# A one-core decoder layer on Trainium2: when x, residuals and weights are asked for at the seams of its stages

## The reference

```python
def reference(x, ctx_1024, mask_BxS2_bf0, ...):
    # two Mamba-2 passes (forward, and over flipped time), joined by a projection:
    #   h = LN(x) + concat(fwd, bwd) @ proj_w.T + proj_b;   attn = LN(h) * ln_w + ln_b
    x = x + _L0_attn_ref(_layernorm(x, axis=-1), ...)
    # 16 heads of 32, queries from LN(x), keys and values from ctx, causal and padding masks
    x = x + _L0_xattn_ref(_layernorm(x, axis=-1), ctx_1024, ctx_1024, mask_BxS2_bf0, ...)
    # mixture of 16 experts: gated q, k, v of width 64, causal attention, gated output
    x = x + _L0_ffn_ref(_layernorm(x, axis=-1), ...)
    return x

def _layernorm(x, axis=-1, eps=1e-05):
    m = jnp.mean(x, axis=axis, keepdims=True)
    v = jnp.var(x, axis=axis, keepdims=True)
    return (x - m) / jnp.sqrt(v + eps)
```

## Time and profile before

| | us |
|---|---|
| median of 3 runs | 4629.91 |
| lowest and highest | 4629.33 and 4635.51 |
| the profiled execution's own time | 4637.03 |
| its span in the trace | 4635.0 |
| mean granted TensorE clock | 0.95 of full |

### The profile page before, as it was taken

One profiled execution on the slowest core, in us unless ns is written; L12 is line 12 of the kernel. 1 busy time (PEld: TensorE's weight loads), 2 busy tenths in 40 slices (PEclk: granted clock), 3 DMA queues, 4 the chain that ended last, 5 costly groups with the idle time before them and its releaser, 6 DMA issues. The chain is left out here.

```text
span 4635.0 us, 72509 instructions
## 1 busy us (share of the span) xinstructions
PE 4139.6 (89%) x26456; PEld 3072.3 (66%) x26456; DVE 3183.5 (69%) x6884; ACT 1664.6 (36%) x3487; POOL 1004.4 (22%) x597
## 2 busy tenths in 40 slices
PE   6999999997898898988858888888898789999998
PEld 5776776764666666656546666566576467777787
DVE  5888888884588887878646646546547476666664
ACT  3333333432333333333226626537437321111111
POOL 1333333242244454444500000000000100000000
PEclk8999999998899999999979999999999899999999
DMA  2111011102011110110143143143142220000000
GB/s 102 35 40 38 26 39 38 40 22 99 17 42 35 45 42 32 49 42 32 36 150 100 42 150 98 61 139 86 62 144 70 78 71 28 28 28 28 28 33 19
DMA packets 144917, 265.89 MB, mean 57 GB/s; under 512 B 25140, under 2 KB 31288, under 8 KB 144568
## 3 DMA queue, kind: packets, MB, share of 16 engines
q1 hardware_dynamic: 144568, 261.27, 17.0%
HBM read 164.58 MB, written 88.08 MB: 55 GB/s over the span
## 5 line engine op out<-in xcount | busy, mean ns | idle before, releaser
L1665 ACT ACTIVATE xa_src<-xa_s,xa_mn 128x896 f32<-128x896 f32 (+7 forms) x512 | 376.7, 738 | 221.8 <-DVE xa_mn L1749 218.4
L1749 DVE TENSOR_REDUCE xa_mn<-xa_s 128x1 f32<-128x896 f32 (+7 forms) x512 | 374.7, 751 | 55.4 <-PE xa_s L1842 49.6
L1848 PE MATMUL xa_gen<-xa_ident,xa_src 128*128 128x128 f32 x2304 | 331.4, 281 | 25.2 <-DVE xa_kq L1774 11.2
L72 PE MATMUL ff_wb<-ff_w_hi,ff_st_hi 128*128 128x512 f32 x768 | 322.5, 420 | 15.7 <-DVE ff_parts L2353 9.9
L1612 POOL TENSOR_TENSOR xa_res<-xa_res,xa_bor 128x512 f32<-128x512 f32 x32 | 40.4, 1267 | 1298.7 <-DMA xa_res<-after_mamba_dram 1298.7
L73 PE MATMUL ff_wb<-ff_w_hi,ff_st_lo 128*128 128x512 f32 x768 | 309.4, 403 | 0.0
L74 PE MATMUL ff_wb<-ff_w_lo,ff_st_hi 128*128 128x512 f32 x768 | 309.3, 403 | 0.0
L1848 PEld LDWEIGHTS xa_gen<-xa_ident,xa_src 128*128 128x128 f32 x2304 | 253.4, 144 | 66.3 <-issue 55.1
L1757 DVE COPY xa_pT<-xa_gen 128x512 f32<-128x512 f32 (+3 forms) x352 | 185.9, 528 | 129.8 <-PE xa_gen L1848 125.8
L1203 PE MATMUL mb_ib<-mb_wc,mb_yT 128*128 128x512 f32 x512 | 268.4, 673 | 1.8 <-DVE mb_y L974 1.0
L2121 POOL TENSOR_TENSOR ff_mixed<-ff_at,ff_rw 128x1024 f32<-128x1024 f32 x32 | 60.9, 1904 | 877.3 <-DVE ff_at L2381 877.3
(11 more groups left out here) (511 smaller groups left out, 11409.4 us busy)
## 6 DMA issues: line engine op xcount, KB each, us to landing
xa_qa<-xa_q_dram SPq DMA_DIRECT2D x384, 64.0 KB, 2.0
xa_q_dram<-xa_kq SPq DMA_DIRECT2D x32, 512.0 KB, 2.8
xa_k_dram<-xa_kq SPq DMA_DIRECT2D x32, 512.0 KB, 2.8
xa_ka<-xa_k_dram SPq DMA_DIRECT2D x192, 64.0 KB, 2.0
xa_st<-xa_k_dram SPq DMA_DIRECT2D x192, 64.0 KB, 2.0
mf_xg<-in_x_dram SPq DMA_DIRECT2D x16, 512.0 KB, 5.4
turned_dram<-mf_xt_hi SPq DMA_DIRECT2D x16, 512.0 KB, 2.6
turned_dram<-mf_xt_lo SPq DMA_DIRECT2D x16, 512.0 KB, 4.0
```

Source lines behind the costliest of these rows:

```text
L72: nc.tensor.matmul(out, w_hi, x_hi, start=first, stop=False)
L1665: a_.activation(pq[:, hh, 0:w], s1[g, i, hh][:, 0:w], ACT.Exp, scale=-1.0, bias=mn[:, i % 2, hh:hh + 1], accum_out=sums[:, i // QT, i % QT ...
L1749: v_.tensor_reduce(mn[:, i % 2, hh:hh + 1], s1[g, i, hh][:, 0:(i + 1) * P], AX.X, ALU.min).then_inc(mx_ready.sem, 1)
L1848: last = tr(ps[:, n * P:(n + 1) * P], pq[:, hh, j * P:(j + 1) * P], ident[:])
```

## The change

Four things change, and no matmul is added or removed.

1. Backward pass, last tile only: its two residuals go to the unused half 0 of `xtok` (function `residual`), and SP asks for them as soon as tile 30's have landed and tile 30 no longer needs that half, and not once tile 30's output is finished.
2. Cross attention, the head of a batch: `load_x`, `stats`, `ln` and `xn` go by halves of 4 tiles. `mask` moves behind them. In the first batch the mask is asked for between the q weights and the k weights. The 1/sqrt chain is run twice per batch on 4 columns.
3. Cross attention, the end of a batch: the first half of x is asked for ahead of output 2, the second ahead of output 3, and the two halves are normed among the outputs. Before `kq` 0 and `kq` 8, PE waits for the low parts of the first 4 tiles alone, and before `kq` 1 and `kq` 9 for the rest.
4. The experts' stage: SP asks for the first two blocks of weights ahead of `load` 1.

```diff
+        def residual(c):
+
+            spare = xtok[:, N % 2, :]
+            return (spare[:, 0:D], spare[:, D:2 * D]) if c == N - 1 else (partb[:], xres[:])
...
-                    wait(sp, out_ready, c - 1)
-                    sp.dma_start(partb[:], part[b, rows, :]).then_inc(res_loaded.sem, 16)
-                    sp.dma_start(xres[:], x_in[b, rows, :]).then_inc(res_loaded.sem, 16)
+                    def load_residual(c):
+                        b, rows = rows_of(c)
+                        for t, src in zip(residual(c), (part, x_in)):
+                            sp.dma_start(t, src[b, rows, :]).then_inc(res_loaded.sem, 16)
+
+                    if c < N - 1:
+                        wait(sp, out_ready, c - 1)
+                        load_residual(c)
+                    if c == N - 2:
+                        wait(sp, base_ready, inner(c))
+                        wait(sp, res_loaded, 2 * c + 1)
+                        load_residual(N - 1)
                 wait(sp, out_ready, c)
...
         def head():
+            yield "load_x", 0
+            yield "load_x", 1
+            for half in range(2):
+                for t in range(QT):
+                    yield "stats", half * QT + t
+                yield "ln", half
+                for t in range(QT):
+                    yield "xn", half * QT + t
             yield "mask", 0
-            yield "load_x", 0
-            for t in range(NT):
-                yield "stats", t
-            yield "ln", 0
...
             yield "load_x", 0, 0
+            yield "load_x", 0, 1
             yield "fetch", 0, 0
+            yield "load_mask", 0, 0
             yield "fetch", 0, 1
...
+                yield "load_x", it + 1, 0
+                yield "o", it, QT - 2
+                yield "load_x", it + 1, 1
+                yield "o", it, QT - 1
+                yield "load_mask", it + 1, 0
+                yield "o", it, QT
+                ahead = [n for n in head() if n[0] != "load_x"]
+                cut, end = ahead.index(("xn", 0)), ahead.index(("ln", 1)) + 1
+                for what, n in ahead[:cut]:
                     yield what, it + 1, n
-                for t in range(QT, QT + 2):
-                    yield "o", it, t
-                for what, n in ahead[2:]:
+                yield "o", it, QT + 1
+                for what, n in ahead[cut:end]:
                     yield what, it + 1, n
-                for t in range(QT + 2, NT):
-                    if ahead:
-                        for i in range(4 * (t - QT - 2), 4 * (t - QT - 2) + 4):
-                            yield "xn", it + 1, i
-                    yield "o", it, t
+                yield "o", it, QT + 2
+                for what, n in ahead[end:]:
+                    yield what, it + 1, n
+                yield "o", it, QT + 3
...
                     if m % (2 * NHG) == 0:
                         if it == 0:
                             pe.wait_ge(half_ready, w + 1)
+                        pe.wait_ge(slo_ready.sem, slo_ready.at(it, w * NT + QT - 1))
+                    if m % (2 * NHG) == 1:
                         pe.wait_ge(slo_ready.sem, slo_ready.at(it, (w + 1) * NT - 1))
...
             yield "xT", 0
+            yield "weights", 0
+            yield "weights", 1
             yield "load", 1
             yield "logits", 0
-            yield "weights", 0
-            yield "weights", 1
```

36 lines of the change are left out of this document (17 added, 19 removed).

## The result

The changed kernel takes 4607.8 us (median of 6 runs, 4604.9 to 4609.6) where the kernel before took 4633.1 beside it (median of 6, 4629.3 to 4638.9): a ratio of 0.9943, with a 95% interval of 0.9931 to 0.9956. It is faster by 25 us. The profiled executions have spans of 4607.9 and 4635.0, 27.1 apart.

What follows compares the result with a forecast made beforehand. PE is busy for most of every stage, so only its waits at seams can be won. Terms A to E, 5.0 + 4.5 + 7.5 + 6.7 + 6.1 = 29.8 us, came off the 4629.9 median: 4600, range 4586 to 4613.

Steps and rivals of the forecast that it cites:

- B: Head of cross attention: norming x by halves starts `kq` 0 sooner, partly given back; 4.5 us (2.9 to 5.5).
- A: End of the backward pass: asking earlier for the last tile's residuals gains 5.0 us (4.7 to 5.3).
- C: Three batch ends of cross attention: earlier x, normed by halves, gains 2.5 us each, 7.5 in all (0 to 21.6).
- rival 3: Cross attention's four q projections: PE's low clock takes back 3.9 us at each, sum 14, 4616 us; chance 0.11.
- Rival 2: Batch ends of cross attention give nothing: residual 4 later, or POOL holds both chains; sum 22.3, 4608 us; chance 0.18.
- D: Four seams from q to k in cross attention: the 1.67 us wait ahead of `kq` 8 goes; 6.7 us (6.0 to 6.8).
- E: Head of the experts' stage: first weights asked for earlier, gating chain starts sooner; 6.1 us (5.1 to 6.5).

Runs made afterwards that it cites:

- the kernel with x later: The changed kernel with each half of x asked for one output later, behind the residuals of outputs 3 and 4; 4594.6 us, ratio 0.9918.
- the shifted kernel: The changed kernel with three spare statistics instructions on DVE at the head of cross attention, so all that follows starts 1.9 us later; 4610.3 us.
- the seam undone: The changed kernel in which `kq` 0 and `kq` 8 wait for all eight low parts again; 4627.1 us, ratio 0.9987.

## Why the prediction was right, and where it was not

The time is 4607.8 for 4600.0, within the range of 4586 to 4613, and the kernel is faster, as given with 0.94. The working is close in four terms, one of them (B) with a step that failed, and wrong in the fifth; the total owes its nearness in part to luck, as said above.

**A** went as worked out: 4.95 for 5.0. ACT, POOL and DVE follow one another as the rows of before said, and the last short instruction beside POOL's add cost what was taken off.

**B** was 3.5 for 4.5, within its ends. Up to the low parts each step was right within 0.4 us: against the 5.0 of part A, the second half's norms were due at 2352.7 and ended at 2353.0, and the q weights' low part was due at 2355.7 and ended at 2356.1. The failed step is the next, "four low parts 2.43 (half of 4.86) give `kq` 0". By it `kq` 0 starts at 2358.3 (its own terms add up to 0.2 less, 2363.1 and not 2363.3); it started at 2360.12, because turns 4 to 7 wait for the first low part's bank and stand ahead of `kq` 0 on PE, at the low clock behind an idle of 8.54 us. The order of PE was in the code, but I read it for the engines that were late (DVE, SP) and not for PE. What the v weights take back was forecast as 2.2; it is 1.2 of the 1.64 that moving their split gave, and the low clock in `kq` 0 cost about 0.6 more.

**C** was 0.2 for 7.5, the failed term. The working had a gain of 3.7 us an end, less 1.2 for POOL's locks. Three of its steps were too small.

Output 4 was to end at 2681.2, which is 15.1 us behind the start of PE's outputs, and ended at 16.2 (2672.00 - 2655.80): 1.1. The step that failed there is the store of output 2, due 9.3 us behind PE's start and landed at 10.9, and residual 4 waits for it. Its cause, small transfers behind x, is borne out by the kernel with x later, which gets 2.0 us an end back in the mean.

The two chains, each held by "up to 1.1" with 1.2 taken for both, were held by 2.1 at the first end, and taking the adds away gives 1.8 an end. And from low part 3 to `kq` 0 the working left 0.9 us (18.9 of DVE against 19.8 to 2701.0), where it is 1.65 (2692.94 to 2694.59), by the banks and PE's order. So at the first end 3.7 - 1.1 - 2.1 - 0.75 is about -0.2, and the trace has -0.2 up to `kq` 0 (17.73 to 17.92). A fourth cost was in rival 3 alone and not in C: the low clock in `kq` 0 takes another 0.6 at this end. The second end shows the same account from the other side: output 4 ended at 15.1, DVE was held by 1.3, and `kq` 0 gained 2.1. Over the three ends `kq` 0 gained 1.9 and the low clock took back 1.8.

Inside the ends "0 and 7.2" I took 2.5 because each cause alone left a gain; together they leave none. Rival 2 ("The batch ends give nothing"), with a chance of 0.18, was the truer case for this term. Its first reason, that residual 4 falls one more transfer back, did not happen; the second, chains held by POOL, is the largest part.

That the new order costs 1.6 us an end in the mean against the old one with the halved wait was in none of my cases. The forecast credited C with the halved wait at `kq` 0 (four low parts in place of eight), so a loss in the order was hidden in the same number. The second chain stood in the working with its full length, but never beside the only thing that it buys, an earlier start: at the first end 4.0 us sooner for 5.5 us more work.

**D** was 7.7 for 6.7. The waits of 1.67 went, and `kq` 8 now starts 0.24 us ahead of the modelled end of the turns (2720.18 + 2.42 against 2722.36). Its twin at `kq` 0 is worth 1.4 to 1.9 us an end with the old order, and 0.9 in the mean with the new one.

**E** was 5.8 for 6.1.

**The bodies** gave 4.4 us that the prediction had at nothing, by the granted clock. Nothing shows that this is the change's doing: between two traces of the changed kernel a single body differs by up to 6.9 us, and the shifted kernel's four sum to 7.0 less. But of before there is one trace, and the two of the changed kernel agree in their sum, so that it is chance is not shown either. Rival 3 looked for the low clock at the batch ends: there the mean is 0.85, 0.88 and 0.85, where before had 0.85, 0.86 and 0.93, and only the first matmuls of `kq` 0 are slow (0.78 us at 2694.59), at a cost of 0.6 us an end in the mean, where the rival had 1.6 to 4.3. So its mechanism is there, at a fraction of its size. The rule of the Trainium skill that I weighed there ("TensorE: Matmul & The Clock Gate", section "HAM oscillation — how this bites in real kernels"), that each burst behind a wait starts slow and pays half of it, agrees for the turns behind the long gap (3.65 us, and 1.91 behind `kq` 0). Behind short gaps the traces go both ways: 3.44 us behind 2.53 of idle in the changed kernel, but 2.03 behind 2.58 with the seam undone. What the low clock can have cost ahead of `kq` 0 is at most the 1.65 us above, and not 3.9.

What stays open: why the granted clock falls inside the bodies, where PE is busy for 87% of the time. The runs show that it moves with the execution; whether it moves with the code as well, they don't, and no view shows its trigger. A and E rest on the traces alone, where their waits are gone; no run undid them.

## What to carry to other kernels

Before a step is credited with starting sooner, look at its whole queue on its own engine and at who frees each buffer that the work ahead of it takes; here a four-bank ring tied PE's turns to DVE's first low part, which stood behind all its other work of the batch end. Halving a step to start its first half sooner pays only by the difference between how much sooner it starts and what the second set-up costs. And measure an edit between marks around it: the batch ends repeated within 0.6 us in two traces of one kernel, and their sum within 1.4 in the kernels that left them alone, while whole runs of one kernel differed by up to 24.

## What the runs showed of the hardware

- A short DVE instruction of four columns that met a POOL add ended only with the add. POOL's adds of the changed kernel at the two places:

```profile
2673.28 1.26 POOL L1636 TENSOR_TENSOR xa_res<-xa_res,xa_bor 128x512 f32<-128x512 f32 x1 [2.00 <-DMA xa_res<-after_mamba_dram]
2676.69 1.26 POOL L1636 TENSOR_TENSOR xa_res<-xa_res,xa_bor 128x512 f32<-128x512 f32 x1 [2.14 <-DMA xa_res<-after_mamba_dram]
2683.50 1.26 POOL L1636 TENSOR_TENSOR xa_res<-xa_res,xa_bor 128x512 f32<-128x512 f32 x1 [5.56 <-DMA xa_res<-after_mamba_dram]
```

The second add ends at 2677.95 and DVE's stretched instruction at 2677.97, the third at 2684.76 and the stretched one at 2684.79. The first add lies beside the statistics of 2671.92 to 2674.38, which took 2.46 us, no more than the 2.47 of the other half beside no add. The Trainium skill ("SBUF — State Buffer", section "SBUF: two separate sides") has a lock held for a whole instruction, against DVE instructions in a two-port mode or with two SBUF inputs; the trace agrees, with 1.0 to 1.1 us for each add that starts just ahead of such an instruction, and none for the statistics, which read one input.
- A 256 KB residual asked for 0.7 us behind 1 MB of x landed 6.2 us after its issue. In the kernel with x later, one asked for ahead of x landed in 2.8 us, and one 2.0 us behind the first half in 4.7. This looks as if transfers on this queue were served in one line; no run tests it further.
- Sixteen turns take 3.65 us behind 8.65 us of idle PE and 1.91 us right behind dense matmuls. Behind some 2.6 us of idle they took 3.44 in one trace and 2.03 in another.
- The granted clock in a body, the same matmuls each time, was between 0.95 and 1.00 over the traces of these kernels, which is 277.6 to 289.0 us. Nothing in these traces says what sets it.
